# Moving ScalarE's rounding of the down weights behind an expert's first tile, with two tiles or more for every expert

## The chip, the cores and the metric

One core of one Trainium2 chip runs the kernel. The metric is device time in microseconds (us), the median of the runs. A core has five engines that run side by side: TensorE (PE in the profile, its weight loads PEld), VectorE (DVE), ScalarE (ACT), GpSimd (POOL) and SyncE (SP), each working through its own instructions in order. Engines wait for each other by semaphores. DMA queues move data between the large memory (HBM) and the on-chip memory (SBUF); TensorE writes its products into another on-chip memory (PSUM).

## The reference, cut to what matters

A block of three parts over x of 8 x 128 tokens with 512 columns: cross attention to a context of 8 x 2048 tokens, causal self attention, and a mixture of experts. The change lies in the third part:

```python
# 1024 tokens, D = 512, F = 1024, E = 8 experts, TOP_K = 2
probs = softmax(xt @ Wg)
topv, topi = top_k(probs, 2);  topv = topv / sum(topv)
cw = zeros(T, E).at[token, topi].set(topv)
h = gelu(einsum('td,edf->tef', xt, Wu))        # up weights, 512 x 1024 for each expert
y = einsum('tef,efd->ted', h, Wd)              # down weights, 1024 x 512 for each expert
moe = einsum('ted,te->td', y, cw)
shared = gelu(xt @ W1) @ W2
return shared + moe                            # and the residual x is added outside
```

## The kernel before

The attention parts fill the first 1246 us of the profile and stay as they are. The function `experts` does the rest.

**Tiles.** A tile is 128 rows of normalised tokens that go through one pair of up and down weights. Tiles 0 to 7 are the shared part (all 1024 tokens; the first six of them run inside the self attention). Each token is also written into the regions of its two experts in a scratch tensor in HBM, so each expert has a list of rows, and its number of tiles follows from the data: one, plus one for each threshold of 128, 256, ... rows that its count exceeds (`thr`, `full`, `n_tiles`). `first` holds the running number of each expert's first tile. The engines read these numbers into registers (`bounds`: `lo` is the first tile of expert e, `hi` the first of the next) and loop over the tiles with a loop whose bounds are known only at run time (`Fori`). Expert tiles are numbered from 8 on below, experts from 0 to 7.

**Split weights.** Products are made to full accuracy from rounded halves: a weight w is split into h, w rounded to the matrix format, and l = w - h; TensorE then multiplies row_h by h, row_l by h and row_h by l. There are two sets of buffers for the parts (`hu`, `hd`, `lu`, `ld`, index s % 2), and one set for the raw weights as they come from HBM (`raw_u`, and `stage` and `raw_e` for the down half). Set s = e + 1 is that of expert e. The weights of one set are 8 chunks of 128 x 1024: four of the up half, four of the down half. During expert e the set s = e + 2 is made, for the expert that follows: ScalarE rounds a chunk (`round_weights`, L2009), GpSimd subtracts (`weights_rest`, L1864), and SyncE then loads the next set's chunk into the raw buffer that came free (`load_raw`, L1833, which waits for the subtraction of the same chunk of the set before).

**One tile, engine by engine.** TensorE (`tile`): the up products (L1943, L1947, then L1955 with the l half), the transposes of the two gelu halves (L1931), which wait for the gelus, the transpose of the next tile's rows (L1904), then the down products (L1967, L1971, L1975). The down products of tile t wait until tile t-1 has been taken out of `down_ps`. ScalarE (`tile`): two gelus out of PSUM (L2015), two roundings of the transposed gelus (L2018), the rounding of the next row tile (L2001), and the DMA that loads a later tile's rows (`load_row`, L1997). VectorE: the rests of these roundings (L2075, L2049), the choice of the weight for each row (L2064 to L2069), and y = down_ps times that weight (L2143). GpSimd (`add_rows`): it waits for y and issues the DMA that adds it to the output (L1871).

**The order around the change.** ScalarE, at the start of each expert e below 7: it reads `first_i[e]`, rounds all 8 chunks of set e + 2, each after its raw chunk has landed (and the down half after `down_done` has reached the tiles before `lo`), then reads the bounds and loops over all tiles of the expert. GpSimd in the same loop already has another order: it subtracts the four up chunks, does `add_rows(lo)`, subtracts the four down chunks, and loops over the tiles from `lo + 1`.

Of the kernel before, what the change touches and what calls it, by code (L numbers as in the profile page):

```python
# [8 lines left out]
ALU = mybir.AluOpType  # L9
ACT = mybir.ActivationFunctionType  # L10
AX_X = mybir.AxisListType.X

P = 128
# [3 lines left out]
B, T, D = 8, 128, 512  # L17
# [4 lines left out]
E, F = 8, 1024  # L22


MAX_TILES = B * T // P + (2 * B * T - E) // P + E
REGION = B * T // P
ROWS = E * REGION + 2
DC = D // P
# [12 lines left out]
CH = 8  # L41
# [12 lines left out]
def weight_chunk(up, down, i):  # L54

    if i < DC:
        return up[:, i, :]
    return down[:, 2 * (i - DC):2 * (i - DC) + 2, :].rearrange("p f n -> p (f n)")
# [1682 lines left out]
def experts(nc, room, stage, on, up_ap, down_ap, out_ap, rows_dram, x2, xn3, logits, hu0, hd0, lu0, ld0,  # L1741
# [7 lines left out]
    with ExitStack() as ctx:  # L1749
        def sb(name, shape, dt=F32):  # L1750
            return ctx.enter_context(nc.sbuf_tensor(name, shape, dt))

        def sem(name):
            return ctx.enter_context(nc.semaphore(name))

        FC = F // P
        NT = B * T // P
# [10 lines left out]
        chosen = sb("chosen", [P, 3])  # L1768
        hold = sb("hold3", [P, MAX_TILES + 1])
        target = sb("target", [P, 1], U32)  # L1770
        tag = sb("tag", [P, MAX_TILES + 2, 4])
        thr = sb("thr", [P, NT - 1])
        full = sb("full", [P, E, NT - 1])
        n_tiles = sb("n_tiles", [P, E])
        first = sb("first", [P, E + 1])
        first_i = sb("first_i", [P, E + 1], U32)
        SEEN = MAX_TILES + 2
        gap = sb("gap", [P, E - 1])
        number = sb("number", [P, SEEN])
        where = sb("where", [P, SEEN])  # L1780
        where_i = sb("where_i", [P, SEEN], U32)
        passed = room[:, 0, 0:SEEN * (E - 1)].rearrange("p (t e) -> p t e", e=E - 1)
        iota = routing.iota
# [8 lines left out]
        consts = sem("consts3")  # L1792
# [3 lines left out]
        where_done = sem("where_done")  # L1796
# [23 lines left out]

        def bounds(eng, e):

            lo = eng.value_load(first_i[0:1, bass.ds(e, 1)], min_val=NT, max_val=MAX_TILES)
            hi = eng.value_load(first_i[0:1, bass.ds(e + 1, 1)], min_val=NT + 1, max_val=MAX_TILES)  # L1824
            return lo, hi

        @block.sync
# [24 lines left out]
        @block.gpsimd  # L1852
        def _(pool):
            pool.memset(hold[:, :], 0.0).then_inc(consts, 1)
            pool.iota(thr[:, :], pattern=[[P, NT - 1]], base=P, channel_multiplier=0,
                      allow_small_or_imprecise_dtypes=True).then_inc(consts, 1)
            pool.iota(number[:, :], pattern=[[1, SEEN]], base=0, channel_multiplier=0,
                      allow_small_or_imprecise_dtypes=True).then_inc(consts, 1)

            def weights_rest(s, chunks):  # L1860

                for i in chunks:
                    pool.wait_ge(hi_done, s * CH + (i + 1))
                    nc.gpsimd.tensor_tensor(weight_chunk(lu[s % 2], ld[s % 2], i), raw_part(i),  # L1864
                                            weight_chunk(hu[s % 2], hd[s % 2], i), ALU.subtract).then_inc(lo_done, 1)

            def add_rows(t):

                pool.wait_ge(y_copied, t + (AHEAD + 1))
                nc.gpsimd.tensor_tensor(hold[:, bass.ds(t, 1)], hold[:, 0:1], hold[:, 0:1], ALU.add)  # L1870
                pool.indirect_dma_start(  # L1871
                    out=out_ap.rearrange("b t d -> (b t) d"),
                    out_offset=bass.IndirectOffsetOnAxis(
                        ap=target[:, :], axis=0),
                    in_=y[:, :], in_offset=None, bounds_check=B * T - 1, oob_is_err=False,
                    compute_op=ALU.add).then_inc(added, 16)

            pool.wait_ge(consts, 3)
            for s in range(NT - 2, NT):
                routing.scatter(pool, s)  # L1880
            pool.wait_ge(firsts_done, 1)
            pool.wait_ge(out_stored, 16 * NT)
            for e in range(E):
                lo, hi = bounds(pool, e)
                if e + 2 <= E:
                    weights_rest(e + 2, range(DC))
                add_rows(lo)
                if e + 2 <= E:
                    weights_rest(e + 2, range(DC, CH))
                with pool.Fori(lo + 1, hi) as t:  # L1890
                    add_rows(t)
            end = pool.value_load(first_i[0:1, E:E + 1], min_val=NT, max_val=MAX_TILES)
            pool.wait_ge(row_in, end * 16 + 32)
            pool.wait_ge(added, end * 16 + NT * 16)
            nc.gpsimd.tensor_tensor(hold[:, 1:2], hold[:, 0:1], hold[:, 0:1], ALU.add)
# [96 lines left out]
        @block.scalar  # L1992
        def _(act):
            def load_row(n):
                place = act.value_load(where_i[0:1, bass.ds(n, 1)], min_val=0, max_val=ROWS - 1)
                act.wait_ge(tag_taken, n)
                act.dma_start(row[:, :], rows_dram[bass.ds(place, 1)].rearrange("o p d -> (o p) d")).then_inc(row_in, 16)  # L1997

            def round_row(n):
                act.wait_ge(rowT_done, n + 1)  # L2000
                nc.scalar.activation(rowT_h[:, :, :], rowT_ps[:, :, :], ACT.Copy).then_inc(rowTh_done, 1)  # L2001

            def round_weights(s, first):

                for i in range(CH):
                    act.wait_ge(raw_in[i], 16 * (s + 1))
                    if i == DC and first is not None:
                        act.wait_ge(down_done, first)
                    nc.scalar.activation(weight_chunk(hu[s % 2], hd[s % 2], i), raw_part(i), ACT.Copy) \  # L2009
                        .then_inc(hi_done, 1)  # L2010

            def tile(t):
                for n in range(NH):
                    act.wait_ge(up_done, t * 2 + (n + 1))
                    nc.scalar.activation(g[:, n, :], up_ps[:, n, :], ACT.Gelu).then_inc(gelu_done, 1)  # L2015
                for n in range(NH):
                    act.wait_ge(gT_done, t * 2 + (n + 1))
                    nc.scalar.activation(gT_h[:, 4 * n:4 * n + 4, :], gT_ps[:, n], ACT.Copy).then_inc(gTh_done, 1)  # L2018
                round_row(t + 1)
                if not isinstance(t, int) or t + 1 == NT:  # L2020
                    load_row(t + 2)

            act.sem_inc(rowTh_done, EARLY + AHEAD)
            act.sem_inc(gelu_done, 2 * EARLY)
            act.sem_inc(gTh_done, 2 * EARLY)
            act.sem_inc(row_in, 16 * NT)
            round_row(EARLY)
            routing.exps(act, NT - 1)
            tile(EARLY)
            round_weights(1, None)  # L2030
            for t in range(EARLY + 1, NT):
                if t + 1 == NT:
                    act.wait_ge(where_done, 1)
                tile(t)
            act.wait_ge(firsts_done, 1)
            for e in range(E):
                if e + 2 <= E:
                    round_weights(e + 2, act.value_load(first_i[0:1, e:e + 1], min_val=NT, max_val=MAX_TILES))
                with act.Fori(*bounds(act, e)) as t:
                    tile(t)  # L2040

        @block.vector
        def _(dve):
            def link(ins):
                routing.link(dve, ins)
# [46 lines left out]
            dve.wait_ge(counted, 1)  # L2092
            link(nc.vector.tensor_tensor(routing.place[:, :], rank_ps[:, :], routing.base[:, :], ALU.add))
            routing.place_rows(dve, NT - 1)
            dve.wait_ge(consts, 3)
            dve.wait_ge(totalled, 1)
            link(nc.vector.memset(first[:, 0:1], float(NT)))
            link(nc.vector.tensor_tensor(full[:, :, :], total_ps[:, 0:E].unsqueeze(2).broadcast_to([P, E, NT - 1]),
# [2 lines left out]
            for e in range(E):  # L2101
# [4 lines left out]
            row_rest(EARLY + 1)  # L2106
            link(nc.vector.scalar_tensor_tensor(out=gap[:, :], in0=first[:, 0:E - 1], scalar=float(REGION),
                                                in1=first[:, 1:E], op0=ALU.add, op1=ALU.subtract))
            link(nc.vector.tensor_tensor(passed, number[:, :].unsqueeze(2).broadcast_to([P, SEEN, E - 1]),
                                         first[:, 1:E].unsqueeze(1).broadcast_to([P, SEEN, E - 1]), ALU.is_ge))  # L2110
            link(nc.vector.tensor_tensor(passed, passed, gap[:, :].unsqueeze(1).broadcast_to([P, SEEN, E - 1]), ALU.mult))
            link(nc.vector.tensor_reduce(where[:, :], passed, AX_X, ALU.add))
            link(nc.vector.scalar_tensor_tensor(out=where[:, :], in0=where[:, :], scalar=-float(NT), in1=number[:, :],
                                                op0=ALU.add, op1=ALU.add))
            nc.vector.tensor_copy(where_i[:, :], where[:, :]).then_inc(where_done, 1)
            add_shared(EARLY)
            def weights_rest(chunks):

# [102 lines left out]
```

## Time and profile before

| what | value |
|---|---|
| median of 3 runs | 1563.64 us (1563.18 to 1564.41) |
| the profiled execution | 1562.89 us, of which the span of the instructions is 1561.1 us |
| TensorE's mean granted clock | 0.993 of full speed |
| busy: PE, ACT, POOL, DVE | 1512.9, 710.6, 705.7, 698.5 us |
| ScalarE's roundings of weights, L2009 | 64 of some 1.05 us each, from 1260.3 us on |

The profile comes from one execution; its times run from the start of its span. "Idle" is time in which an engine had nothing in hand before an instruction, and the arrow behind it names what released it. The view of stretches gives the busy time of each engine between two points of time, the granted clock (1.00 is full speed) and the share of the DMA engines' time in use.

### The profile page before, as it was taken

To read this page: it belongs to the slowest core of one execution; us is meant where nothing else is said; L and a number is where in the kernel's file an instruction comes from. 1 tells how busy PE (TensorE), PEld (TensorE's weight loads), DVE (VectorE), ACT (ScalarE), POOL (GpSimd) and SP (SyncE) were. 2 spreads that over 40 slices of the span, in tenths; PEclk is the share of its full clock that TensorE was granted. 3 is DMA by queue.
4 is the path that set the end of the run, shared out by engine and by line. 5 is a ranking of instruction groups with operands and counts; after the bars stand their busy time and mean duration, and the time that the engine had idled before them with its cause. 6 is when DMAs were issued, how large, how long until landed. Compare 5 with 4: busy or idle time off the path is not lost. (4 is left out here: it accounts for less than half of the span.)

```text
span 1561.1 us, 25710 instructions
## 1 busy us (share of the span) xinstructions
PE 1512.9 (97%) x10070; PEld 1220.1 (78%) x10071; DVE 698.5 (45%) x1098; ACT 710.6 (46%) x1197; POOL 705.7 (45%) x558
## 2 busy tenths in 40 slices
PE   7999999999999999999999999999899899999997
PEld 5678888888888888888888888765577678877786
DVE  4124533533632731822722633562555555555442
ACT  3244544544543644544544454423566464444521
POOL 3112931941851652572481491167311107687751
PEclk9999999999999999999999999999999999999999
DMA  6111041031022114104103104025000185566411
GB/s 215 61 55 47 15 129 35 28 104 60 28 81 77 35 34 123 35 29 124 40 29 102 61 7 144 1 99 173 14 28 28 38 300 150 154 192 188 140 36 36
DMA packets 57445, 127.84 MB, mean 82 GB/s; under 512 B 7104, under 2 KB 11264, under 8 KB 57344
## 3 DMA queue, kind: packets, MB, share of 16 engines
q1 hardware_dynamic: 48672, 109.81, 21.7%
q0 software_dynamic: 4304, 8.44, 2.8%
q10 hardware_dynamic: 4368, 8.18, 1.7%
q8 instruction: 71, 1.16, 0.3%
q14 instruction: 30, 0.25, 0.1%
HBM read 94.22 MB, written 33.24 MB: 82 GB/s over the span
## 5 line engine op out<-in xcount | busy, mean ns | idle before, releaser
L299 POOL TENSOR_TENSOR ctx_l<-stage,ctx_h 128x1024 fp32r<-128x1024 f32 x62 | 147.5, 2403 | 481.4 <-ACT ctx_h L666 481.3
L366 PE MATMUL pair_ps<-wv,ctx_h 128*128 128x512 f32 x1024 | 324.1, 398 | 9.3 <-DVE ctx_l L736 9.2
L366 PE MATMUL pair_ps<-ctx_h,wk 128*128 128x512 f32 x1024 | 331.2, 394 | 0.0
L774 DVE TENSOR_TENSOR s_top<-ps_s,s_top 128x512 f32<-128x512 f32 x192 | 121.2, 684 | 338.7 <-ACT s L635 338.7
L366 PEld LDWEIGHTS pair_ps<-wv,ctx_h 128*128 128x128 f32 x1024 | 188.2, 189 | 53.0 <-issue 10.0
L366 PEld LDWEIGHTS pair_ps<-ctx_h,wk 128*128 128x128 f32 x1024 | 192.2, 188 | 42.7 <-issue 1.2
L617 ACT ACTIVATE vt<-pair_ps 128x512 f32<-128x512 f32 x128 | 76.5, 598 | 275.2 <-PE pair_ps L366 214.0
L366 PE MATMUL pair_ps<-wv,ctx_l 128*128 128x512 f32 x512 | 200.6, 392 | 0.0
L366 PE MATMUL pair_ps<-ctx_l,wk 128*128 128x512 f32 x512 | 199.5, 390 | 0.0
L635 ACT ACTIVATE s<-ps_s 128x512 f32<-128x512 f32 x256 | 133.0, 602 | 61.1 <-PE ps_s L419 36.7
L611 ACT ACTIVATE kT<-pair_ps 128x512 f32<-128x512 f32 x128 | 76.5, 598 | 176.8 <-PE pair_ps L366 176.8
L419 PEld LDWEIGHTS ps_s<-qT,kT 64*128 64x128 f32 x2048 | 119.3, 188 | 19.2 <-issue 16.5
L419 PE MATMUL ps_s<-qT,kT 64*128 64x128 f32 x2048 | 131.5, 278 | 0.0
L642 ACT ACTIVATE s<-s 128x1024 f32<-128x1024 f32 x128 | 125.7, 1049 | 4.6 <-DVE s L804 4.6
L776 DVE COPY s_top<-ps_s 128x512 f32<-128x512 f32 x64 | 40.4, 685 | 175.2 <-ACT s L635 175.2
L448 PEld LDWEIGHTS ps_o<-s,vt 128*64 128x64 f32 x2048 | 111.6, 137 | 5.0 <-issue 2.8
L448 PE MATMUL ps_o<-s,vt 128*64 128x128 f32 x2048 | 114.2, 273 | 1.2 <-ACT s L642 1.2
L366 PEld LDWEIGHTS pair_ps<-wv,ctx_l 128*128 128x128 f32 x512 | 96.7, 189 | 20.8
L366 PEld LDWEIGHTS pair_ps<-ctx_l,wk 128*128 128x128 f32 x512 | 96.2, 188 | 19.8 <-issue 1.2
L804 DVE TENSOR_TENSOR s<-s,ps_s 128x2048 f32<-128x2048 f32 x48 | 106.1, 2275 | 0.0
L2015 ACT ACTIVATE wxo<-pair_ps 128x512 f32<-128x512 f32 x46 | 27.1, 598 | 148.5 <-PE pair_ps L1955 147.0
L1864 POOL TENSOR_TENSOR lu<-raw_u,hu 128x1024 fp32r<-128x1024 f32 x28 | 68.8, 2788 | 27.3 <-issue 27.3
(291 smaller groups left out, 2313.4 us busy)
## 6 DMA issues: line engine op xcount, KB each, us to landing
stage<-in_ctx_dram SPq DMA_DIRECT2D x64, 512.0 KB, 4.2
rows_scratch<-bo SPq DMA_DIRECT2D x66, 258.5 KB, 4.9
raw_u<-in_up_dram SPq DMA_DIRECT2D x32, 512.0 KB, 4.2
stage<-in_down_dram SPq DMA_DIRECT2D x16, 512.0 KB, 4.0
raw_e<-in_down_dram SPq DMA_DIRECT2D x16, 512.0 KB, 4.0
bo<-rows_scratch ACTq DMA_DIRECT2D x22, 258.5 KB, 3.0
s<-in_x_dram SPq DMA_DIRECT2D x2, 1024.0 KB, 11.2
q_scratch<-s SPq DMA_DIRECT2D x2, 1024.0 KB, 4.6
```

Source lines behind the costliest of these rows:

```text
L299: nc.gpsimd.tensor_tensor(lo, raw, hi, ALU.subtract).then_inc(done, 1)
L366: mm = nc.tensor.matmul(out, w(c), m(c), start=(c + k == 0), stop=(c == DC - 1 and k == 2))
L419: mm = nc.tensor.matmul(ps_e[:, 2 * (n % 2) + e, i], kT[rows, p, i * P:(i + 1) * P], qT[rows, p, :], start=True, stop=True)
L448: mm = nc.tensor.matmul(ps_o[e * XD:(e + 1) * XD, p, :], vt[:, (b * MT + t) % RING, h * XD:(h + 1) * XD], s[:, h, t, :], start=(t == 0), s ...
L611: nc.scalar.activation(kT[:, p, :], ps_p[:, NTH[b, "K", g, p] % 2], ACT.Copy).then_inc(k_copied, 1)
L617: nc.scalar.activation(vt[:, nth_v(b, g, t) % RING, :], ps_p[:, NTH[b, "V", g, t] % 2], ACT.Copy) \
L635: nc.scalar.activation(s[:, 2 * p + e, 4 * g:4 * g + 4, :], ps_e[:, 2 * (n % 2) + e], ACT.Copy) \
L642: nc.scalar.activation(part, part, ACT.Exp, scale=X_SCALE).then_inc(exp_done, 1)
L774: ins = nc.vector.tensor_tensor(top[:, p, e], bank, top[:, p, e], ALU.max)
L776: ins = nc.vector.tensor_copy(top[:, p, e], bank)
L804: nc.vector.tensor_tensor(s[:, h], s[:, h], largest_score, ALU.subtract).then_inc(shifted, 1)
L1864: nc.gpsimd.tensor_tensor(weight_chunk(lu[s % 2], ld[s % 2], i), raw_part(i), weight_chunk(hu[s % 2], hd[s % 2], i), ALU.subtract).then_in ...
```

## The change

Four things are changed, all in the expert part.

- ScalarE reads both bounds of an expert first, rounds the four up chunks, then does the first tile `lo`, then rounds the four down chunks, and loops over the tiles from `lo + 1`.
- The first threshold becomes -1, which every count exceeds, so that every expert has at least two tiles; an added second tile would hold blank rows, which the DMA that adds to the output drops.
- The largest number of tiles grows from 31 to 40, and with it the small tables `hold`, `tag` and `where_i`; the bounds that the register loads declare change with it.
- `number` and `where` are no longer tiles of their own but lie at the end of `room[:, 0]`. GpSimd waits for its first two constants, writes the -1 and counts one constant more; two waits for `consts` go from 3 to 4.

```diff
--- before.py
+++ after.py
@@ -22,7 +22,7 @@
 E, F = 8, 1024
 
 
-MAX_TILES = B * T // P + (2 * B * T - E) // P + E
+MAX_TILES = B * T // P + 2 * B * T // P + 2 * E
 REGION = B * T // P
 ROWS = E * REGION + 2
 DC = D // P
@@ -1776,8 +1776,7 @@
         first_i = sb("first_i", [P, E + 1], U32)
         SEEN = MAX_TILES + 2
         gap = sb("gap", [P, E - 1])
-        number = sb("number", [P, SEEN])
-        where = sb("where", [P, SEEN])
+        number, where = room[:, 0, D - 2 * SEEN:D - SEEN], room[:, 0, D - SEEN:D]
         where_i = sb("where_i", [P, SEEN], U32)
         passed = room[:, 0, 0:SEEN * (E - 1)].rearrange("p (t e) -> p t e", e=E - 1)
         iota = routing.iota
@@ -1820,8 +1819,8 @@
 
         def bounds(eng, e):
 
-            lo = eng.value_load(first_i[0:1, bass.ds(e, 1)], min_val=NT, max_val=MAX_TILES)
-            hi = eng.value_load(first_i[0:1, bass.ds(e + 1, 1)], min_val=NT + 1, max_val=MAX_TILES)
+            lo = eng.value_load(first_i[0:1, bass.ds(e, 1)], min_val=NT, max_val=MAX_TILES - 2)
+            hi = eng.value_load(first_i[0:1, bass.ds(e + 1, 1)], min_val=NT + 2, max_val=MAX_TILES)
             return lo, hi
 
         @block.sync
@@ -1854,7 +1853,9 @@
             pool.memset(hold[:, :], 0.0).then_inc(consts, 1)
             pool.iota(thr[:, :], pattern=[[P, NT - 1]], base=P, channel_multiplier=0,
                       allow_small_or_imprecise_dtypes=True).then_inc(consts, 1)
-            pool.iota(number[:, :], pattern=[[1, SEEN]], base=0, channel_multiplier=0,
+            pool.wait_ge(consts, 2)
+            pool.memset(thr[:, 0:1], -1.0).then_inc(consts, 1)
+            pool.iota(number, pattern=[[1, SEEN]], base=0, channel_multiplier=0,
                       allow_small_or_imprecise_dtypes=True).then_inc(consts, 1)
 
             def weights_rest(s, chunks):
@@ -1875,7 +1876,7 @@
                     in_=y[:, :], in_offset=None, bounds_check=B * T - 1, oob_is_err=False,
                     compute_op=ALU.add).then_inc(added, 16)
 
-            pool.wait_ge(consts, 3)
+            pool.wait_ge(consts, 4)
             for s in range(NT - 2, NT):
                 routing.scatter(pool, s)
             pool.wait_ge(firsts_done, 1)
@@ -2000,9 +2001,9 @@
                 act.wait_ge(rowT_done, n + 1)
                 nc.scalar.activation(rowT_h[:, :, :], rowT_ps[:, :, :], ACT.Copy).then_inc(rowTh_done, 1)
 
-            def round_weights(s, first):
-
-                for i in range(CH):
+            def round_weights(s, first, chunks=range(CH)):
+
+                for i in chunks:
                     act.wait_ge(raw_in[i], 16 * (s + 1))
                     if i == DC and first is not None:
                         act.wait_ge(down_done, first)
@@ -2034,9 +2035,13 @@
                 tile(t)
             act.wait_ge(firsts_done, 1)
             for e in range(E):
+                lo, hi = bounds(act, e)
                 if e + 2 <= E:
-                    round_weights(e + 2, act.value_load(first_i[0:1, e:e + 1], min_val=NT, max_val=MAX_TILES))
-                with act.Fori(*bounds(act, e)) as t:
+                    round_weights(e + 2, lo, range(DC))
+                tile(lo)
+                if e + 2 <= E:
+                    round_weights(e + 2, lo, range(DC, CH))
+                with act.Fori(lo + 1, hi) as t:
                     tile(t)
 
         @block.vector
@@ -2092,7 +2097,7 @@
             dve.wait_ge(counted, 1)
             link(nc.vector.tensor_tensor(routing.place[:, :], rank_ps[:, :], routing.base[:, :], ALU.add))
             routing.place_rows(dve, NT - 1)
-            dve.wait_ge(consts, 3)
+            dve.wait_ge(consts, 4)
             dve.wait_ge(totalled, 1)
             link(nc.vector.memset(first[:, 0:1], float(NT)))
             link(nc.vector.tensor_tensor(full[:, :, :], total_ps[:, 0:E].unsqueeze(2).broadcast_to([P, E, NT - 1]),
@@ -2106,13 +2111,13 @@
             row_rest(EARLY + 1)
             link(nc.vector.scalar_tensor_tensor(out=gap[:, :], in0=first[:, 0:E - 1], scalar=float(REGION),
                                                 in1=first[:, 1:E], op0=ALU.add, op1=ALU.subtract))
-            link(nc.vector.tensor_tensor(passed, number[:, :].unsqueeze(2).broadcast_to([P, SEEN, E - 1]),
+            link(nc.vector.tensor_tensor(passed, number.unsqueeze(2).broadcast_to([P, SEEN, E - 1]),
                                          first[:, 1:E].unsqueeze(1).broadcast_to([P, SEEN, E - 1]), ALU.is_ge))
             link(nc.vector.tensor_tensor(passed, passed, gap[:, :].unsqueeze(1).broadcast_to([P, SEEN, E - 1]), ALU.mult))
-            link(nc.vector.tensor_reduce(where[:, :], passed, AX_X, ALU.add))
-            link(nc.vector.scalar_tensor_tensor(out=where[:, :], in0=where[:, :], scalar=-float(NT), in1=number[:, :],
+            link(nc.vector.tensor_reduce(where, passed, AX_X, ALU.add))
+            link(nc.vector.scalar_tensor_tensor(out=where, in0=where, scalar=-float(NT), in1=number,
                                                 op0=ALU.add, op1=ALU.add))
-            nc.vector.tensor_copy(where_i[:, :], where[:, :]).then_inc(where_done, 1)
+            nc.vector.tensor_copy(where_i[:, :], where).then_inc(where_done, 1)
             add_shared(EARLY)
             def weights_rest(chunks):
```

## Rows read from the trace of the kernel before

**Rows 1.** The page, part 1: engine, busy us (share of the span), instructions
```profile
PE 1512.9 (97%) x10070; PEld 1220.1 (78%) x10071; DVE 698.5 (45%) x1098; ACT 710.6 (46%) x1197; POOL 705.7 (45%) x558
```

**Rows 2.** Who waited for whom, 1270:1561: us in total, times, longest
```profile
PE gT_ps L1931 <- ACT wxo L2015: 8.7, 4, 3.1
ACT hd L2009 <- DMA raw_e<-in_down_dram: 7.3, 7, 1.5
```

**Rows 3.** Stretches: length, busy PE, PEld, DVE, ACT, POOL, clock, DMA
```profile
1277.20:1293.22 16.02, 12.91 (x62) 10.24 (x60) 7.10 (x9) 7.37 (x10) 6.25 (x3) 1.00 0.59 200
...
1356.01:1368.76 12.75, 12.75 (x61) 10.26 (x60) 6.53 (x8) 6.94 (x10) 10.76 (x6) 1.00 0.43 134
1381.52:1395.95 14.43, 12.62 (x62) 10.22 (x60) 7.77 (x11) 7.14 (x10) 12.18 (x7) 1.00 0.66 201
1408.39:1422.48 14.09, 12.90 (x61) 10.26 (x60) 7.79 (x10) 7.06 (x10) 12.00 (x7) 1.00 0.67 210
...
1472.81:1489.69 16.88, 14.32 (x61) 11.49 (x60) 8.14 (x11) 7.21 (x10) 13.04 (x7) 0.90 0.33 94
1515.20:1527.63 12.43, 12.43 (x61) 10.21 (x60) 3.90 (x9) 2.77 (x5) 1.75 (x2) 1.00 0.14 27
```

**Rows 4.** Timeline, TensorE, 1480:1487: start, us, line, [idle before <-releaser]
```profile
1481.15 0.66 PE L1931 MATMUL gT_ps<-on,wxo 128*128 128x128 f32 x4 [2.56 <-ACT wxo L2015]
...
1482.66 3.45 PE L1967 MATMUL down_ps<-hd,gT_h 128*128 128x512 f32 x8
```

**Rows 5.** One stretch of 1 us, columns as in rows 3
```profile
1483.00:1484.00 1.00, 1.00 (x4) 0.81 (x3) 0.49 (x2) 0.95 (x2) 1.00 (x2) 0.50 0.00 0
```

**Rows 6.** The chain that ended last, 1464:1490: start, us, what
```profile
1464.67 10.06 POOL ld L1864 x4
...
1474.74 3.83 DMA raw_e<-in_down_dram
```

**Rows 7.** Timeline, ScalarE, 1360:1391
```profile
1364.03 0.34 ACTq L1997 DMA_DIRECT2D bo<-rows_scratch  x1
1373.65 0.60 ACT L2015 ACTIVATE wxo<-pair_ps 128x512 f32<-128x512 f32 x1 [9.38 <-PE pair_ps L1955]
...
1377.86 3.91 ACT L2009 ACTIVATE hu<-raw_u 128x1024 fp32r<-128x1024 f32 x4 [0.83 <-issue]
...
1386.80 1.06 ACT L2009 ACTIVATE hd<-raw_e 128x1024 fp32r<-128x1024 f32 x1 [1.46 <-DMA raw_e<-in_down_dram]
1388.30 1.09 ACT L2015 ACTIVATE wxo<-pair_ps 128x512 f32<-128x512 f32 x2 [0.44 <-issue]
```

**Rows 8.** Timeline, GpSimd, 1280:1430
```profile
1286.97 9.46 POOL L1864 TENSOR_TENSOR lu<-raw_u,hu 128x1024 fp32r<-128x1024 f32 x4 [27.28 <-issue]
...
1302.57 5.26 POOL L1864 TENSOR_TENSOR ld<-raw_e,hd 128x1024 fp32r<-128x1024 f32 x2
...
1372.46 5.32 POOL L1864 TENSOR_TENSOR ld<-stage,hd 128x1024 fp32r<-128x1024 f32 x2
...
1425.70 5.29 POOL L1864 TENSOR_TENSOR ld<-stage,hd 128x1024 fp32r<-128x1024 f32 x2
```

**Rows 9.** Timeline, VectorE, 1300:1438
```profile
1302.58 5.28 DVE L2066 SCALAR_TENSOR_TENSOR chosen<-tag,chosen 128x1 f32 x1
...
1308.34 0.75 DVE L2143 TENSOR_SCALAR wxo<-down_ps,chosen 128x512 f32<-128x512 f32 x1
...
1436.18 0.75 DVE L2143 TENSOR_SCALAR wxo<-down_ps,chosen 128x512 f32<-128x512 f32 x1
```

**Rows 10.** Timeline, TensorE, 1312:1446
```profile
1313.02 2.11 PE L1967 MATMUL down_ps<-hd,gT_h 128*128 128x512 f32 x8
...
1442.28 2.11 PE L1967 MATMUL down_ps<-hd,gT_h 128*128 128x512 f32 x8
```

**Rows 11.** Line L2015 (ScalarE) in one stretch: length, busy (x count), clock, DMA
```profile
1356.01:1381.52 25.51, 2.40 (x4) 1.00 0.55 158
```

**Rows 12.** Timeline, GpSimd, 1246:1260
```profile
1257.46 0.96 POOL L1735 DMA_INDIRECT rows_scratch<-xn,slot_i  x1 [7.71 <-DVE slot_i L1720]
```

## The prediction

> **What bounds the kernel now.** Read the page's busy shares first: TensorE is busy for 1512.9 of 1561.1 us, the three others below half [rows 1]. So time can only come from TensorE's idle places or from its clock. Next the table of waits for the expert part (from 1270 us): TensorE has one kind of idle there, 8.7 us in 4 times before the transposes of the gelus, released by the gelu on ScalarE [rows 2]. Behind it stands ScalarE's own wait for the raw down weights, 7.3 us. Then the stretches, one for each expert's first tile [rows 3]. A first tile that nothing disturbs takes 12.75 us for an even expert and 12.43 us for an odd one (1356.01 and 1515.20; the two stretches left out, experts 1 and 5, are odd and take 12.44 and 12.43, by differences of their own bounds). Four are longer: 16.02 (expert 0), 14.43 (3), 14.09 (4), 16.88 (6). The chain before the last of them shows how [rows 6]: GpSimd subtracts the old set's down chunks for 10.06 us, only then does SyncE load the next raw chunks, the last lands 3.83 us later, ScalarE rounds it and only then starts the gelu. On ScalarE's own timeline in expert 3 the last rounding starts at 1386.80 and the gelu at 1388.30, both halves back to back, which says that both had been ready [rows 7].
>
> **The sum.** The down half of the rounding is moved behind the first tile's ScalarE work. In its place nothing is left ahead of the gelu but the four up chunks, 3.91 us from 1377.86, done at 1381.77 in expert 3 [rows 7], where TensorE starts that tile's up products only at 1381.52 [rows 3] and asks for a gelu some 5 us later. So in all four tiles the wait goes, and each falls back to the length of its parity:
> 16.02 - 12.75 = 3.27; 14.43 - 12.43 = 2.00; 14.09 - 12.75 = 1.34; 16.88 - 12.75 = 4.13; together 10.74 us.
> The last one is more than its gap: 2.56 us idle, and then the eight down products take 3.45 us [rows 4] where eight take 2.11 us elsewhere [rows 10]. [...] TensorE had been idle just before, so I count those 1.34 us and what is lost around them with the gap. The idle of 3.1 us in expert 0 left the clock at 1.00 [rows 2, 3], so it is not certain: without it the sum would be 9.4.
> [...]
>
> The profiled execution took 1562.89 us, of which 1561.1 is the span; it becomes 1552.15. The median of the runs is 0.75 above it: 1563.64 - 10.74 = 1552.90.
>
> **What the moved part costs where it now stands.** After a first tile ScalarE ends with the load of a row tile; in expert 2 that is 1364.03 to 1364.37. A rounding has started 0.83 us after such a load [rows 7], so the four down chunks would run from about 1365.2 to 1369.1 (four at the up half's pace of 0.98), and the next gelu is asked for at 1373.65 after an idle of 9.38 us [rows 7]: a margin of 4.5. For the stalled experts the shift of TensorE moves both alike. Raw chunks are no limit any more: in expert 3 the last one had landed by 1386.80, and its rounding now comes after the tile's ScalarE work, about 1387 to 1391. Cost nothing; if the cover failed, each us of lateness would be a us on TensorE.
> GpSimd's down subtraction starts after y of the first tile, at 1372.46 in expert 2 [rows 8], 3.4 us after the rounding would end. Nothing.
> The wait for `down_done` stands behind the tile that needed it: already met. The 64 roundings, the loads (SyncE's queue keeps its order and its waits for the subtraction) and their DMAs stay as many as they are. ScalarE reads both bounds before the up chunks: one register load fewer in each expert, some tenths either way, with about 4 us free before the gelu.
>
> **What is late next.** GpSimd. From expert 2's down subtraction at 1372.46 to expert 4's at 1425.70 are four steps of 13.31 us, each four chunks and one `add_rows` [rows 8], while TensorE wants a tile every 12.43 or 12.75. VectorE hangs on it: the small operation L2066 at 1302.58 lasts 5.28 us and ends at 1307.86, just when GpSimd's run, that began its last pair at 1302.57 for 5.26 us, is over [rows 8, 9]. So y of a tile comes some 1.3 us after GpSimd's run, and the down products of the next tile need it.
> Tightest at the start: in expert 0 GpSimd's first run starts at 1286.97 after an idle of its own [rows 8], not for the rounding (the hu chunks had been there for long) but, by the code, for the stored shared output. It doesn't move when TensorE gains 3.27. So y of tile 9 stays at 1308.34 + 0.75 = 1309.09, and tile 10's down products move from 1313.02 to 1309.75 [rows 9, 10]: 0.66 us left.
> In experts 2 to 4: everything, GpSimd too, moves by 3.27 at expert 1, whose last tile has GpSimd waiting. Then TensorE gains 2.00 and 1.34 more, which GpSimd doesn't follow. y of tile 19 at 1436.18 + 0.75 - 3.27 = 1433.66, the down products of tile 20 at 1442.28 - 6.61 = 1435.67 [rows 9, 10]: 2.0 us left. In expert 6 GpSimd has waited for TensorE, and there is more room. So I put this at zero, with an upper end of 5 us (half of the gain) for small shifts of VectorE's blocked operations, and a lower end of zero: nothing here can speed up more than the stalls.
>
> **Two tiles or more.** Does any expert have one tile? A tile is two gelus. The shortest expert stretches (2, 3 and 5) have four gelus, one is shown [rows 11]; the eight give 6, 6, 4, 4, 6, 4, 6, 6, which is 21 tiles. So no tile is added. Had one been, it would cost 12.43 to 12.75 us [rows 3].
>
> **Tables and constants.** GpSimd gets a wait and a memset before its first scatter, below 1 us; its last scatter waits 7.71 us for VectorE anyway [rows 12], and the loads of rows wait for that one. `passed` grows from 231 to 294 elements in two VectorE operations and a reduction, tenths of a us beside TensorE's tile 6. Zero; bounds 0 and +0.5.
>
> **The rivals.**
> 1. The wait changes its owner: GpSimd with VectorE takes over where it had 0.7 and 2.0 us left. For it: rows 8 and 9. Against: both margins are positive without any luck. If it eats a third to a half, 3 to 5 us: 1556 to 1558. Chance 0.16.
> 2. The clock's fall is not of the gap: 1563.64 - 9.4 = 1554.2, if it comes again elsewhere. Chance 0.14; the forecast's mechanism else holds.
> 3. Nothing gained, because ScalarE's first tile meets another wait of the same length, such as the row load at its end that waits for VectorE's tags. Against it: in undisturbed experts that load follows at once. 1563.6. Chance 0.04.
> 4. Slower. Place: the second tile's gelu, now behind the down chunks on ScalarE. Price: from the point at which the last raw chunk lands more than 4.5 us after ScalarE is free for it, every us is one of TensorE, in each of 7 experts. It decides against the change when these sum to more than 10.74, 1.5 each, that is landings some 6 us later than the margin's start. At 2 us each: 1563.64 - 10.74 + 14 = 1566.9. Against: the landing took 3.83 us [rows 6] and lies before the place. Chance 0.03.
>
> **The numbers.** Forecast, 0.63: 1552.9, its own range 1551.5 to 1554 (the runs differ by 1.2, and other executions may have lost more to the clock than the profiled one did). With rivals 1 and 2 the range goes from 1551.0 to 1557.0 and leaves out rivals 3 and 4 and the far end of rival 1. This kernel's runs can't tell less than about 0.2%, 3.1 us, from no change. Faster by more: 0.63 + 0.16 + 0.14 = 0.93; same 0.04; slower 0.03.
>
> **What would show it.** After: the eight first-tile stretches at 12.4 and 12.75 us; no wait of L1931 for L2015 on TensorE beyond tenths; no clock of 0.5 after 1260 us; on ScalarE four roundings before and four after a first tile's row load, the latter with no wait for a DMA; GpSimd's runs as long as now; 21 expert tiles. Wrong if TensorE idles before L1967 or L1971 (rival 1), if L2015 of a second tile comes right behind L2009 (rival 4), or if first tiles keep their gap (rival 3).

## The result, and the profile after

| | median | runs | profiled execution: time, span |
|---|---|---|---|
| before | 1563.41 us | 4: 1562.97 to 1564.41 | 1562.89, 1561.1 us |
| changed | 1552.47 us | 4: 1551.81 to 1553.17 | 1553.17, 1551.4 us |

The ratio is 0.9927, with an interval from 0.9915 to 0.994: 10.9 us faster, with 1552.9 forecast. The spans differ by 9.7 us only. From the start of expert 0's first tile to the start of the last tile it was 1277.20 to 1540.07, 262.87 us, and is 1278.56 to 1530.52, 251.96 us: 10.91 less. But the first of these tiles starts 1.36 us later than before: this was lost in the attention part, which the change doesn't touch. The place can be read from the two traces. After the same idle time of 2.35 us the same 16 products take 7.10 us before the change and 8.80 after it; from 1040 to 1042 us the granted clock is 1.00 in the first and 0.50 in the second:

```profile
1039.34 7.10 PE L1158 MATMUL bank<-wxo,stage 128*128 128x512 f32 x16 [2.35 <-PEq L75]
...
1039.41 8.80 PE L1158 MATMUL bank<-wxo,stage 128*128 128x512 f32 x16 [2.35 <-PEq L75]
```

The changed kernel's four runs stand in two pairs 1.3 us apart (1551.81, 1551.85; 1553.10, 1553.17), and the profiled one is of the upper pair. One such fall of the clock would explain the distance, but the other three runs have no trace, so this is not shown.

The page's busy shares [rows 1] of the changed kernel:

```profile
PE 1510.8 (97%) x10070; PEld 1218.5 (79%) x10071; DVE 714.3 (46%) x1098; ACT 709.6 (46%) x1197; POOL 705.9 (46%) x559
```

The waits of its expert part [rows 2], us in total, times, longest. TensorE has no row of its own any more; its weight loads wait 0.2 us for each tile's gelu, as every undisturbed tile did, and ScalarE waits for TensorE before 44 gelus instead of 37:

```profile
ACT wxo L2016 <- PE pair_ps L1956: 135.4, 44, 9.4
...
PEld gT_ps L1932 <- ACT wxo L2016: 4.4, 22, 0.3
```

The first tiles of experts 0, 2, 3, 4, 6 and 7 in the changed kernel, columns as in [rows 3]. The second number is TensorE's busy time, and it fills each stretch; the clock is 1.00 in all:

```profile
1278.56:1291.30 12.74, 12.74 (x61) 10.26 (x60) 6.52 (x9) 7.58 (x10) 3.02 (x2) 1.00 0.59 205
1354.04:1366.78 12.74, 12.74 (x61) 10.25 (x60) 6.88 (x8) 7.60 (x10) 10.75 (x6) 1.00 0.45 130
1379.53:1391.93 12.40, 12.40 (x61) 10.21 (x60) 7.92 (x10) 7.48 (x10) 10.43 (x7) 1.00 0.66 197
1404.37:1417.11 12.74, 12.74 (x62) 10.26 (x61) 9.72 (x10) 7.53 (x10) 10.77 (x7) 1.00 0.73 195
1467.46:1480.21 12.75, 12.75 (x61) 10.26 (x60) 8.65 (x10) 7.64 (x11) 10.76 (x7) 1.00 0.44 125
1505.71:1518.13 12.42, 12.42 (x61) 10.22 (x60) 3.91 (x9) 2.77 (x5) 1.74 (x2) 1.00 0.12 27
```

ScalarE in expert 3, changed [rows 7]. Four roundings, the gelu after an idle of 3.93 us (it waits for TensorE now, not the other way round), the row load, four roundings without a wait for a DMA, and 4.94 us idle before the second tile's gelu:

```profile
1376.43 3.90 ACT L2010 ACTIVATE hu<-raw_u 128x1024 fp32r<-128x1024 f32 x4 [1.40 <-issue]
1384.27 0.60 ACT L2016 ACTIVATE wxo<-pair_ps 128x512 f32<-128x512 f32 x1 [3.93 <-PE pair_ps L1956]
...
1387.37 0.34 ACTq L1998 DMA_DIRECT2D bo<-rows_scratch  x1
1387.82 2.01 ACT L2010 ACTIVATE hd<-stage 128x1024 fp32r<-128x1024 f32 x2 [0.21 <-issue]
1389.73 1.99 ACT L2010 ACTIVATE hd<-raw_e 128x1024 fp32r<-128x1024 f32 x2
1396.66 0.60 ACT L2016 ACTIVATE wxo<-pair_ps 128x512 f32<-128x512 f32 x1 [4.94 <-PE pair_ps L1956]
```

GpSimd, VectorE and TensorE, changed, the rows that answer to [rows 8 to 10]:

```profile
1288.28 9.46 POOL L1865 TENSOR_TENSOR lu<-raw_u,hu 128x1024 fp32r<-128x1024 f32 x4 [27.21 <-ACT hd L2010]
...
1303.88 5.26 POOL L1865 TENSOR_TENSOR ld<-raw_e,hd 128x1024 fp32r<-128x1024 f32 x2
1310.60 0.19 POOL L1871 TENSOR_TENSOR hold<-hold 128x1 f32 x1 [1.46 <-DVE wxo L2148]
...
1370.49 5.32 POOL L1865 TENSOR_TENSOR ld<-stage,hd 128x1024 fp32r<-128x1024 f32 x2
...
1423.45 2.97 POOL L1865 TENSOR_TENSOR ld<-stage,hd 128x1024 fp32r<-128x1024 f32 x1
```

```profile
1300.66 8.51 DVE L2071 SCALAR_TENSOR_TENSOR chosen<-tag,chosen 128x1 f32 x1
...
1309.66 0.75 DVE L2148 TENSOR_SCALAR wxo<-down_ps,chosen 128x512 f32<-128x512 f32 x1
...
1433.97 0.75 DVE L2148 TENSOR_SCALAR wxo<-down_ps,chosen 128x512 f32<-128x512 f32 x1
```

```profile
1311.10 2.10 PE L1968 MATMUL down_ps<-hd,gT_h 128*128 128x512 f32 x8
...
1436.91 2.12 PE L1968 MATMUL down_ps<-hd,gT_h 128*128 128x512 f32 x8
```

y of tile 9 is done at 1309.66 + 0.75 = 1310.41, and tile 10's down products start at 1311.10: 0.69 us of margin, 0.66 forecast. y of tile 19 at 1434.72, tile 20's down products at 1436.91: 2.19, 2.0 forecast. GpSimd's step is (1423.45 - 1370.49) / 4 = 13.24 us, against 13.31 before.

### The profile page after: what moved, and what is told of

Same layout as the page of the kernel before. It is cut to its first block and busy times, and to the rows that moved or that the text cites. A ratio compares the mean times of both kernels' runs of the same rounds, so it can differ in the third digit from the quotient of the medians.

```text
span 1551.4 us, 25674 instructions
## 1 busy us (share of the span) xinstructions
PE 1510.8 (97%) x10070; PEld 1218.5 (79%) x10071; DVE 714.3 (46%) x1098; ACT 709.6 (46%) x1197; POOL 705.9 (46%) x559
```

## The experiments

Theory: the gelu of four first tiles stood behind the rounding of raw down chunks that had not landed; the change takes the landing out of its way, and what then covers the moved rounding is ScalarE's idle time before the second tile. Rivals: the tables or the code around give the gain; ScalarE's busy time was the price; GpSimd, at 46%, is or isn't the next bound. Runs of one group shared one chip and its runs of the kernel before.

| run | median | before, same chip | ratio (95%) |
|---|---|---|---|
| order_only | 1553.76 | 1564.97 | 0.9936 (0.992 to 0.9953) |
| tables_only | 1564.1 | 1564.97 | 0.9998 (0.9989 to 1.0008) |
| order_125 | 1561.0 | 1564.97 | 0.9978 (0.9968 to 0.9987) |
| last_two | 1552.34 | 1564.97 | 0.9923 (0.9906 to 0.9939) |
| round_2x | 1553.76 | 1564.9 | 0.9926 (0.991 to 0.9943) |
| round_3x | 1586.61 | 1564.9 | 1.0128 (1.011 to 1.0146) |
| pool_extra | 1554.09 | 1564.9 | 0.9927 (0.9911 to 0.9944) |
| align_experts | 1552.8 | 1564.9 | 0.992 (0.9903 to 0.9936) |
| pool_more | 1562.93 | 1564.72 | 0.999 (0.9981 to 0.9999) |
| pool_gap | 1553.49 | 1564.72 | 0.9927 (0.9912 to 0.9942) |
| align_all | 1553.46 | 1564.72 | 0.9926 (0.9913 to 0.994) |

### The order alone, the rest alone

`order_only` is the kernel before with ScalarE's new loop; `tables_only` is the changed kernel with the old loop:

```diff
-                lo, hi = bounds(act, e)
                 if e + 2 <= E:
-                    round_weights(e + 2, lo, range(DC))
-                tile(lo)
-                if e + 2 <= E:
-                    round_weights(e + 2, lo, range(DC, CH))
-                with act.Fori(lo + 1, hi) as t:
+                    round_weights(e + 2, act.value_load(first_i[0:1, e:e + 1], min_val=NT, max_val=MAX_TILES))
+                with act.Fori(*bounds(act, e)) as t:
                     tile(t)
```

> The kernel before with ScalarE's new order alone: thresholds, table sizes and the place of number and where stay as they were. Theory (the gelu of a first tile stood behind the rounding of raw down chunks that had not landed): the whole gain, ratio 0.993 to the kernel before, 1552.5 us, first tiles of experts 0, 3, 4 and 6 at 12.75, 12.43, 12.75 and 12.75 us. Rival (part of the gain is of the tables, the constants or the code around them): between 1553.5 and 1563.

> The changed kernel with ScalarE's old order: two tiles for every expert, larger tables and the moved tiles stay. Theory: 1563.4 us, ratio 1.000, 21 expert tiles, the four long first tiles back (16.0, 14.4, 14.1 and 15.5 to 16.9 us). On the clock: if TensorE's fall to the lower level in expert 6 belongs to the idle gap in front of it, a fall can show again behind one of the four gaps and nowhere else after 1260 us; if it has a cause of its own, it shows at a place without a gap. Rival (the tables cost or give something): off by more than 1 us.

The order alone gives the gain (its first tiles of experts 0, 3, 4 and 6 take 12.73, 12.44, 12.74 and 12.74 us), and the rest gives and costs nothing: 21 expert tiles, as before. The four long first tiles are back in `tables_only`, 15.99, 14.13, 14.48 and 16.97; the first and the last of them:

```profile
1277.32:1293.31 15.99, 12.90 (x61) 10.25 (x60) 7.08 (x9) 7.37 (x10) 6.26 (x3) 1.00 0.63 201
...
1472.98:1489.95 16.97, 14.33 (x61) 11.48 (x60) 8.36 (x11) 7.20 (x10) 13.05 (x7) 0.90 0.35 93
```

### The order in the experts that had no gap

```diff
+                behind = e in (1, 2, 5)
-                    round_weights(e + 2, lo, range(DC))
+                    round_weights(e + 2, lo, range(DC if behind else CH))
                 tile(lo)
-                if e + 2 <= E:
+                if e + 2 <= E and behind:
```

> The changed kernel, but with the down half of the rounding behind the first tile in experts 1, 2 and 5 alone, the three whose first tiles waited for nothing before; in experts 0, 3, 4 and 6 all eight chunks stand ahead of it again. Theory: nothing gained, 1563.4 us, ratio 1.000, the four gaps as before. Rival (every expert gains a little, since four roundings of 0.95 us leave ScalarE's way to the gelu): 3/7 of the gain, 1558.7 us.

The forecast missed: the ratio is 0.9978, and its interval leaves 1.000 out. It doesn't leave out the rival's 0.997 (1558.7 us), so the ratio alone can't decide between the two, but the tiles can. The first tiles of experts 1, 2 and 5 gained nothing: they take 12.42, 12.74 and 12.42 us, and took 12.44, 12.75 and 12.43 before. Expert 2's:

```profile
1357.45:1370.19 12.74, 12.74 (x61) 10.26 (x60) 6.53 (x8) 7.61 (x10) 10.75 (x6) 1.00 0.46 130
```

The four other first tiles take 15.80, 13.82, 14.54 and 14.62 us, 58.78 together against 61.57 in `tables_only`, and most of it is expert 6's:

```profile
1278.90:1294.70 15.80, 12.89 (x61) 10.25 (x60) 7.11 (x9) 7.84 (x10) 5.94 (x3) 1.00 0.65 200
...
1474.06:1488.68 14.62, 12.88 (x61) 10.24 (x60) 8.60 (x10) 7.61 (x10) 12.63 (x7) 1.00 0.40 109
```

The last rounding and the gelus of expert 6 in `tables_only`, then in `order_125`:

```profile
1478.88 1.06 ACT L2010 ACTIVATE hd<-raw_e 128x1024 fp32r<-128x1024 f32 x1 [1.39 <-DMA raw_e<-in_down_dram]
1480.74 1.09 ACT L2016 ACTIVATE wxo<-pair_ps 128x512 f32<-128x512 f32 x2 [0.81 <-issue]
```

```profile
1479.97 1.06 ACT L2010 ACTIVATE hd<-raw_e 128x1024 fp32r<-128x1024 f32 x1 [1.34 <-DMA raw_e<-in_down_dram]
1480.94 1.06 ACT L2016 ACTIVATE wxo<-pair_ps 128x512 f32<-128x512 f32 x2
```

From the start of the last rounding to the gelu it is 1.86 us in the one and 0.97 in the other. The register loads of the bounds, which the old order has between the two, stand ahead of all roundings here. This shortens TensorE's gap from 2.64 to 1.74 us, and the clock's fall behind it is gone (1.00 instead of 0.90 in the stretch). In experts 0, 3 and 4 the same stretch of ScalarE goes from 1.24, 1.47 and 1.72 us to 0.97 as well, so the loads cost 0.3 to 0.9 us in front of a gelu. But TensorE's gaps there go only from 3.09 to 2.91, 1.51 to 1.21 and 1.58 to 1.63 us: the last chunk's rounding started later in these tiles, by 0.12, 0.23 and 0.83 us, and took part of it back, in expert 4 all. So the new order holds two parts, the register loads ahead of the roundings and the down half behind the first tile, and by the tiles the first alone is worth 61.57 - 58.78 = 2.8 of the 10.9 us, most of it in expert 6.

### Landing or busy time

```diff
-                    round_weights(e + 2, lo, range(DC))
+                    round_weights(e + 2, lo, range(DC + 2))
...
-                    round_weights(e + 2, lo, range(DC, CH))
+                    round_weights(e + 2, lo, range(DC + 2, CH))
```

> The changed kernel with six chunks ahead of the first tile and only the last two (those of raw_e) behind it. Theory (the landing of the last raw chunks is the price, not the 0.95 us of a rounding): the first two down chunks are rounded 0.6 to 2.7 us before the gelu is asked for, also in experts 0, 3, 4 and 6, so the whole gain stays: 1552.5 us, ratio 0.993. Rival (the price is ScalarE's busy time ahead of the gelu): half the gain, 1558 us.

The whole gain with two chunks moved instead of four. ScalarE in expert 3: the two chunks of `stage` are done before TensorE is ready for a gelu, which still comes after 2.02 us of idle (in expert 0 only 0.37 us are left):

```profile
1379.08 1.99 ACT L2010 ACTIVATE hd<-stage 128x1024 fp32r<-128x1024 f32 x2
1383.09 0.60 ACT L2016 ACTIVATE wxo<-pair_ps 128x512 f32<-128x512 f32 x1 [2.02 <-PE pair_ps L1956]
...
1386.58 2.01 ACT L2010 ACTIVATE hd<-raw_e 128x1024 fp32r<-128x1024 f32 x2 [0.16 <-issue]
```

### How much the moved part may cost

```diff
+                    for _ in range(1 if i >= DC and s > 1 else 0):     # 2 in round_3x
+                        again[0] += 1
+                        nc.scalar.activation(weight_chunk(hu[s % 2], hd[s % 2], i), raw_part(i), ACT.Copy) \
+                            .then_inc(repeated, 1)
+                        act.wait_ge(repeated, again[0])
                     nc.scalar.activation(weight_chunk(hu[s % 2], hd[s % 2], i), raw_part(i), ACT.Copy) \
```

> The changed kernel with each down chunk rounded twice by ScalarE in all seven experts that prepare weights (the same values, one wait between the two): some 4.3 us more of ScalarE behind the first tile. Its idle time before the second tile's gelu was 4.9 to 5.2 us in the changed kernel. Theory (that idle time is a cover, and a cost of the moved part shows only past it): no change against the changed kernel within 1 us, 1552.5. Rival (ScalarE's added work costs as it goes, for instance through GpSimd, which takes the chunks): 5 us or more.

> The same with each down chunk rounded three times: some 8.6 us more behind the first tile. Theory: the cover of 4.9 to 5.2 us is used up, and the rest, some 3.5 us in each of seven experts, delays the second tile's gelu: 1552.5 + 24 = 1576 us (1570 to 1582), slower than the kernel before, with the second tiles at 16 instead of 12.6 us. Rival (ScalarE's work behind the first tile is free): 1552.5.

Double stays within the cover: 0.45 to 0.90 us of idle are left before the second tiles' gelus. Triple goes past it, and by more than forecast: seven tiles of TensorE are longer by 5.96, 4.89, 3.30, 5.05, 5.07, 6.15 and 3.27 us, 33.7 together. Their gaps are alike, 3.11 to 3.48 us and 23.2 together; around five of them (3.16 and more) the clock falls to 0.5, and around two (3.11 and 3.14) it doesn't. Two of the gaps, in experts 1 (1345.09) and 2, and a microsecond at each (the clock is the third number from the end):

```profile
1345.09 1.12 PE L1934 MATMUL gT_ps<-on,wxo 128*128 128x128 f32 x4 [3.42 <-ACT wxo L2023]
...
1387.44 0.66 PE L1934 MATMUL gT_ps<-on,wxo 128*128 128x128 f32 x4 [3.14 <-ACT wxo L2023]
```

```profile
1345.00:1346.00 1.00, 0.91 (x5) 0.91 (x6) 0.00 (x0) 0.52 (x2) 1.00 (x2) 0.50 0.97 367
1387.00:1388.00 1.00, 0.56 (x5) 0.56 (x6) 0.00 (x0) 0.87 (x2) 1.00 (x2) 1.00 1.02 340
```

So the forecast's 3.5 us for a gap holds, and the rest, 33.7 - 23.2 = 10.5 us, is the clock's.

### GpSimd and VectorE

`pool_extra` puts one more subtraction ahead of each run of four chunks, with a wait for it behind:

```diff
                     pool.wait_ge(hi_done, s * CH + (i + 1))
+                    if i % DC == 0:
+                        again[0] += 1
+                        nc.gpsimd.tensor_tensor(weight_chunk(lu[s % 2], ld[s % 2], i)[:, 0:512],
+                                                raw_part(i)[:, 0:512],
+                                                weight_chunk(hu[s % 2], hd[s % 2], i)[:, 0:512],
+                                                ALU.subtract).then_inc(repeated, 1)
+                        pool.wait_ge(repeated, again[0])
```

> The changed kernel with one more subtraction of 128 x 512 on GpSimd at the head of each run of four chunks, some 1.25 us, 14 times, 17.5 us of GpSimd in all. Theory (GpSimd with VectorE is next, with the margins measured in the changed kernel: 0.69 us before tile 10's down products, 2.19 before tile 20's): tile 10 loses 2.5 - 0.7 = 1.8, tiles 18 to 20 together 5.3, tiles 24 and 25 together 2.0; 1552.5 + 9.1 = 1561.6 us (1558 to 1564), and TensorE's idle time stands before the down products. Rival (GpSimd at 46% busy has room): no change, 1552.5. Other end (all of it on the path): 1570.

The forecast of 1561.6 us missed: no time was lost. VectorE in tile 9, then GpSimd:

```profile
1301.80 1.82 DVE L2080 SCALAR_TENSOR_TENSOR chosen<-tag,chosen 128x1 f32 x1 [0.15 <-DVE chosen L2078]
1303.77 2.35 DVE L2083 SCALAR_TENSOR_TENSOR chosen<-tag,chosen 128x1 f32<-128x1 f32 x1
...
1306.43 0.75 DVE L2157 TENSOR_SCALAR wxo<-down_ps,chosen 128x512 f32<-128x512 f32 x1
```

```profile
1301.71 1.88 POOL L1869 TENSOR_TENSOR ld<-stage,hd 128x512 fp32r<-128x512 f32 x1
1303.68 4.81 POOL L1874 TENSOR_TENSOR ld<-stage,hd 128x1024 fp32r<-128x1024 f32 x2
1308.44 4.74 POOL L1874 TENSOR_TENSOR ld<-raw_e,hd 128x1024 fp32r<-128x1024 f32 x2
1313.13 0.19 POOL L1880 TENSOR_TENSOR hold<-hold 128x1 f32 x1
```

The held operation that lasted 8.51 us in the changed kernel (1300.66) ends here after 1.82 us, at 1303.62, in the pause between GpSimd's extra subtraction (done at 1303.59) and the next. y comes at 1307.18 instead of behind the run, so `add_rows` at 1313.13 has nothing to wait for, where it waited 1.46 us in the changed kernel. The pause gave back what the subtraction cost. Two more runs take this apart. `pool_more` has the same work with no pause (the result goes to unused room, and the wait is for the extra subtraction of the run before); `pool_gap` has the pause and no work:

```diff
+                    if i % DC == 0:                                     # pool_more
+                        pool.wait_ge(repeated, again[0])
+                        again[0] += 1
+                        nc.gpsimd.tensor_tensor(room[:, 0, :], raw_part(i)[:, 0:512],
+                                                weight_chunk(hu[s % 2], hd[s % 2], i)[:, 0:512],
+                                                ALU.subtract).then_inc(repeated, 1)
...
+                    if i % DC == 1:                                     # pool_gap
+                        pool.wait_ge(lo_done, s * CH + i)
```

> The changed kernel with one more subtraction of 128 x 512 on GpSimd at the head of each of the 14 runs of four chunks, as in the run with an extra subtraction before, but written to unused room and with no wait behind it, so that the run stays without a pause: some 1.2 us each. Theory A (a pause in GpSimd's run lets VectorE's held operation through, and that pause, not spare time, hid the cost before; with no pause the margins of 0.69 and 2.19 us decide): tile 10 loses 1.7, tiles 18 to 20 5.0, tiles 24 and 25 1.8, together 8.5: 1561 us (1558 to 1563), TensorE idle before the down products. Theory B (GpSimd has spare time, the margins mean nothing): 1552.5 to 1554.

> The changed kernel with nothing added but one wait of GpSimd, in each run of four chunks, for its own first chunk. Theory A: VectorE's held operation (L2071, 8.51 us for tile 9 in the changed kernel) ends at that pause, y of tile 9 comes before GpSimd's run is over, so its wait of 1.45 us behind each run goes, GpSimd's step falls from 13.3 to about 12 us, and the margins before tiles 10 and 20 grow from 0.69 and 2.19 to over 3 us; the time stays, since TensorE waits for none of it: 1552.5, within 1.5. Theory B (the operation is not held by GpSimd's run): margins as they were, and the same time.

`pool_more` is as theory A says. VectorE's operation is held for 11.57 us, TensorE idles before the down products, and the waits add to 8.9 us in 6 places. The tiles grow by 2.47 (10), 2.27, 1.33, 1.67 (18 to 20), 0.60 and 1.67 (24, 25), 10.0 together, with 8.5 forecast:

```profile
1301.64 11.57 DVE L2080 SCALAR_TENSOR_TENSOR chosen<-tag,chosen 128x1 f32 x1 [0.15 <-DVE chosen L2078]
...
1313.70 0.75 DVE L2157 TENSOR_SCALAR wxo<-down_ps,chosen 128x512 f32<-128x512 f32 x1
```

```profile
1314.51 2.14 PE L1977 MATMUL down_ps<-hd,gT_h 128*128 128x512 f32 x8 [2.36 <-DVE wxo L2157]
```

```profile
PE down_ps L1977 <- DVE wxo L2157: 8.9, 6, 2.4
```

`pool_gap`: y of tile 9 is done at 1306.43, and the margins before tiles 10 and 20 grow to 4.82 and 5.11 us. The time is that of the changed kernel. One part of theory A missed: GpSimd's step falls to (1420.91 - 1370.38) / 4 = 12.63 us and not to 12, since a wait of some 0.98 us for y stays behind most of its runs. VectorE shows why:

```profile
1300.81 1.91 DVE L2073 SCALAR_TENSOR_TENSOR chosen<-tag,chosen 128x1 f32 x1
1302.88 2.42 DVE L2076 SCALAR_TENSOR_TENSOR chosen<-tag,chosen 128x1 f32<-128x1 f32 x1 [0.15 <-DVE chosen L2073]
...
1305.68 0.75 DVE L2150 TENSOR_SCALAR wxo<-down_ps,chosen 128x512 f32<-128x512 f32 x1
1306.35 1.32 DVE L2061 COPY tag<-bo 128x4 f32 x1
```

The pause ends the first hold, but the next small operation (0.22 us in tile 9 of the changed kernel) is held for 2.42 us and the copy of the tags (0.16 there) for 1.32. Each of the three ends within 0.03 us of the end of one of GpSimd's subtractions (1302.70, 1305.28, 1307.64), although GpSimd waits for its own work only at the first. `pool_extra` shows the same three (1.82, 2.35 and 1.41 us).

### Where the weights lie

```diff
+        sb("pad", [P, 8])                      # align_experts, align_all; one more ahead of wk in align_all
         hu = [hu0, sb("hu1", [P, DC, F], F32R)]
```

`align_experts` has an unused tile of 32 bytes in each partition ahead of `hu1`, which with `hd1`, `lu1` and `ld1` holds the weights of even experts. `align_all` has this tile and a second one ahead of `wk` in the cross attention.

> [...] Even experts' tiles take 12.75 us, odd ones' 12.43. Theory (the place in SBUF slows the products): even tiles fall to 12.43, 11 or 12 tiles of 0.32 us, 1552.5 - 3.7 = 1548.8 us. Rival (the place in the loop's code, or something else): no change, 1552.5.

> [...] In the expert part alone this took a product of 128 x 512 from 0.2343 to 0.2335 us, start to start. Theory (the same in the cross attention, where such products take 0.234 as well): some 8,000 products by 0.0008 us are 6.5 us less, 1546 us, faster than the changed kernel. Rival (those products' pace has another limit there): 1552.

Both miss. An even expert's tile falls from 12.75 to 12.71 us and not to 12.43:

```profile
1291.86:1304.57 12.71, 12.71 (x61) 10.21 (x60) 6.66 (x8) 2.77 (x5) 12.56 (x8) 1.00 0.80 217
```

Eleven such tiles are 0.4 us, which the runs can't show. In `align_all` the premise of 0.234 us for such products in the cross attention was wrong too: over nearly 3,000 of them the median distance from start to start is 0.227 us in the changed kernel already, and 0.227 in `align_all`. The traces hold no addresses, so no run shows where in SBUF the tiles start.

## Why the prediction was right

The sum. Four first tiles were to fall back to the length of their parity, 10.74 us; they did, each within 0.03 us, and the experts' part lost 10.91. That the order alone did it is shown by the first pair of runs, and that the landing of the last two raw chunks was the price by `last_two`; the part of the register loads is told under `order_125`. That the medians differ by 10.94 us, 0.2 from the sum, is in part luck: runs of one kernel lie 1.3 us and more apart, and expert 6's share rests on a fall of the clock that had been seen in one execution.

The clock (rival 2). The forecast counted 1.34 us and more of expert 6, where the granted clock was 0.50 from 1483 to 1484 us [rows 5], with its gap, and gave 0.14 to a fall of its own. That was the author's estimate, from this one fall and one long gap without a fall. The runs bear the forecast out in the expert part: from 1262 us to the end of the last tile, every fall in the traces of before, `tables_only`, `order_125`, `round_3x` and the changed kernel begins in a gap of TensorE or within 1.1 us of its end (gaps of 2.56 and 2.64 us in expert 6, five of 3.16 to 3.48 in `round_3x`), and none is seen without one. Length alone doesn't decide: gaps of 3.11, 3.09 and 2.91 us in expert 0 (before, `tables_only`, `order_125`) and of 3.11 and 3.14 in `round_3x` left it at 1.00, and the idle of 2.35 us at 1039 us was followed by a fall to 0.50 in the changed kernel and by none in the kernel before, in code that is the same. So in these traces a gap brings the risk of a fall and not the fall, and what decides stays open. The 1.34 us could have been missing from the gain in an execution without that fall.

The cover. The forecast was 4.5 us, and ScalarE's idle before the seven second tiles' gelus is 4.83 to 5.27. The rounding starts 0.1 us after the row load and not 0.83: the 0.83 belonged to the register loads, which come before the up chunks now (1.36 to 1.40 us idle there, 1.93 in expert 5). That term was mis-sized on the safe side. What the prediction called "some tenths either way" for the register loads is 0.3 to 0.9 us where a gelu waits behind them, as `order_125` shows; in the changed kernel none does.

Rivals 1, 3 and 4. GpSimd was rightly named as next, with margins right to 0.2 us, and `pool_more` shows that they decide: 1.2 us more in each run take 10 us. The change itself used up most of them: from y of tile 9 to tile 10's down products it was 1313.02 - 1309.09 = 3.93 us before, and 0.69 is left; for tile 20 it was 1442.28 - 1436.93 = 5.35, and 2.19 is left [rows 9, 10]. Neither went below zero, so no time was lost. No new wait took the place of the old one (rival 3). Rival 4's mechanism exists, and `round_3x` shows its price, but it begins only with some 5 us more on ScalarE.

Two tiles and tables. No tile was added and no cost found, 0.9998.

## What to carry to other kernels

If an engine prepares the next stage's data in front of this stage's work, look at which of its inputs lands last, and put that part behind the first piece of this stage's work; it need not be all of it. Read the next bound by margins (when it delivers, when it is needed), not by its busy share: GpSimd at 46% had 0.69 us left. And before adding work to test such a margin, see that the test doesn't add a pause: here the same subtraction took no time with a pause (`pool_extra`, 1554.09 us) and 10 us without one (`pool_more`, 1562.93).

## What the hardware showed that was not expected

- In these traces a VectorE operation on 128 x 1 in SBUF (L2071 of the changed kernel) is held while GpSimd runs subtractions back to back. In tile 9 it lasts 8.51 us in the changed kernel and 11.57 in `pool_more`, past several boundaries between subtractions, against 0.22 us in tile 10 of both, where no subtraction runs. One semaphore wait of GpSimd for its own instruction let it through, after 1.91 us in `pool_gap` and 1.82 in `pool_extra`. Behind that wait other small operations of tile 9 are held too, but each only to the next boundary: 2.42 us for L2076 (128 x 1) and 1.32 us for the copy of the tags (128 x 4) in `pool_gap`. The subtractions themselves look different there: in the changed kernel the four records of the run of tile 9 overlap by 0.57 to 0.59 us, behind the wait in `pool_gap` by 0.04. Whether this is why the boundaries let an operation through stays open. Not every operation is held: in the changed kernel the subtractions out of PSUM (L2080 there) keep their 0.69 us beside the same runs of GpSimd, and the comparison L2069 (128 x 1) its 0.20 to 0.21.
- In the changed kernel the 24 up products of tile 9 (even expert) take 5.62 us, 0.234 from start to start (1291.30 to 1296.92), those of tile 11 (odd) 5.45 us, 0.227 (1316.79 to 1322.24). With 32 unused bytes in each partition ahead of the even experts' weights, tile 9's take 5.60 us, 0.233 (1291.86 to 1297.46 in `align_experts`), and all eleven even tiles 12.70 to 12.71 us instead of 12.74 to 12.75. So the added room has an effect, but it is a small part of the difference. The traces hold no addresses; why it has one and where the rest comes from stay open, and no other place was tried.
